# First attention stage of a four-stage decoder kernel: largest scores ahead of P's split, P turned right behind the value products, row tiles turned by VectorE and transfers instead of TensorE

## The reference

```
x = x + tanh(g_xattn[0]) * L0_xattn(layernorm(x), ctx)   # attention, 16 heads in 8 pairs
x = x + tanh(g_ffn[0])   * L0_ffn(layernorm(x))          # feed-forward with 8 low-rank experts, top 2
x = x + tanh(g_xattn[1]) * L1_xattn(layernorm(x), ctx)   # causal attention
x = x + tanh(g_ffn[1])   * L1_ffn(layernorm(x))          # mixture of 8 low-rank maps

# L0_xattn, for a batch b of 128 rows and a head h (Wq, w_kc_q, W_qr folded to one 512x64 matrix A_h):
q_r    = x_b @ A_h                     # 128 x 64
k_r    = rope(ctx_b) @ W_kr[h]         # 128 x 64
P      = softmax(q_r @ k_r.T)          # 128 x 128
out_b += P @ rope(ctx_b) @ G_h         # G_h = w_kc_kv[h].T @ Wo's rows of h: 128 x 512
```

## Time and profile before

| | |
|---|---|
| median of 3 runs | 1375.35 us (1373.85 to 1378.79) |
| the profiled execution | 1376.7 us, of which the span is 1374.9 us |
| granted TensorE clock, mean | 0.997 of full speed |
| busy: PE, DVE, ACT, POOL | 1348.0, 929.3, 518.5, 422.1 us |

### The profile page before, as it was taken

How to read it: one execution, slowest core, us unless ns; L and a number is a source line. 1 busy time by engine, 2 the same in 40 slices (tenths; PEclk the granted TensorE clock), 3 DMA queues, 4 the chain that set the end, 5 groups by cost and what they waited for, 6 DMA issues and landing times.

```text
span 1374.9 us, 20467 instructions
## 1 busy us (share of the span) xinstructions
PE 1348.0 (98%) x7596; PEld 1091.5 (79%) x7596; DVE 929.3 (68%) x1787; ACT 518.5 (38%) x1569; POOL 422.1 (31%) x463
## 2 busy tenths in 40 slices
PE   7899999999999999999999999999999999999999
PEld 6688888888778788878887888788876788887787
DVE  5565675666674877786678667776988777845533
ACT  2544455445464331231113111311127777822220
POOL 3123433233254443101111112113427865630000
PEclk9999999999999999999999999999999999999999
DMA  8633434433454322210121112112334031144431
GB/s 282 222 124 101 148 124 130 131 123 116 135 149 120 92 85 77 88 47 20 43 88 31 51 39 85 43 46 69 106 102 136 28 129 62 47 139 153 139 123 54
DMA packets 108615, 138.35 MB, mean 101 GB/s; under 512 B 12876, under 2 KB 66252, under 8 KB 108516
## 3 DMA queue, kind: packets, MB, share of 16 engines
q1 hardware_dynamic: 108516, 137.05, 31.3%
HBM read 97.15 MB, written 39.85 MB: 100 GB/s over the span
## 4 chain that ended last, share of the span: by engine, by line
PE 81%; DVE 9%; DMA 5%; ACT 2%; issue 1%; SPq 1%; POOL 1%; DVEq 0%; ACTq 0%; POOLq 0%
PE bank L118 78%; PE bank L121 4%; DMA PYZ<-pscr 2%; DMA pscr<-PYZ 2%; SPq L170 1%; DVE PYZ L164 1%; DVE XR L140 1%; DVE AH L130 1%; DVE STG L130 1%; DVE AH L127 1%; DVE st L152 1%; ACT Pb L124 1%; ACT PT L124 1%; DMA XR<-scr 0%; DVE XR L137 0%
## 5 line engine op out<-in xcount | busy, mean ns | idle before, releaser
L118 PE MATMUL bank<-XT,AR 128*128 128x512 f32 x1152 | 280.2, 393 | 0.1
L118 PE MATMUL bank<-AR 128*128 128x512 f32 x1056 | 260.6, 396 | 3.2 <-DVE Msb L127 2.3
L118 PEld LDWEIGHTS bank<-XT,AR 128*128 128x128 f32 x1152 | 213.9, 188 | 48.3 <-issue 1.5
L124 ACT ACTIVATE STG<-bank,b1c 128x512 f32<-128x512 f32 x128 | 88.3, 690 | 387.7 <-PE bank L118 317.7
L118 PEld LDWEIGHTS bank<-AR 128*128 128x128 f32 x1056 | 193.7, 188 | 48.2 <-DVE Msb L127 2.7
L118 PE MATMUL bank<-AR,CT 128*128 128x512 f32 x768 | 192.7, 394 | 0.0
L118 PE MATMUL bank<-AR,AH 128*128 128x512 f32 x768 | 185.9, 390 | 0.0
L127 DVE CAST AH<-STG 128x512 fp32r<-128x512 f32 x192 | 93.8, 488 | 110.5 <-PE bank L118 96.4
L118 PEld LDWEIGHTS bank<-AR,AH 128*128 128x128 f32 x768 | 143.7, 188 | 30.7 <-issue 1.1
L118 PEld LDWEIGHTS bank<-AR,CT 128*128 128x128 f32 x768 | 140.0, 188 | 27.2 <-issue 0.4
L127 POOL CAST BA<-STG 128x256 fp32r<-128x256 f32 x64 | 31.4, 490 | 396.4 <-PE bank L118 242.8
(11 more groups left out here) (139 smaller groups left out, 1839.3 us busy)
## 6 DMA issues: line engine op xcount, KB each, us to landing
XR<-scr SPq DMA_DIRECT2D x64, 256.0 KB, 2.9
pscr<-PYZ SPq DMA_DIRECT2D x30, 512.0 KB, 2.9
PYZ<-pscr SPq DMA_DIRECT2D x120, 128.0 KB, 2.9
XR<-in_x_dram SPq DMA_DIRECT2D x32, 256.0 KB, 3.6
scr<-XR SPq DMA_DIRECT2D x32, 256.0 KB, 2.1
STG<-in_WoT_dram SPq DMA_DIRECT2D x8, 512.0 KB, 3.9
STG<-in_Wq_dram SPq DMA_DIRECT2D x8, 512.0 KB, 4.9
STG<-in_W1L_dram SPq DMA_DIRECT2D x16, 256.0 KB, 2.7
```

Source lines behind the costliest of these rows:

```text
L118: return self.e.matmul(o, w, x, start=start, stop=stop, skip_group_check=True) if self.e else Nothing()
L124: return self.e.activation(o, x, func, **kw) if self.e else Nothing()
```

## The change

Five things change, all in the first stage.

- `by_blocks` also holds for the row tiles of (0, 1), (0, 2), (0, 3) and (1, 0). TensorE's 16 `ln_turn` in the steps (64 transposes) go. VectorE gets `ln_blocks` behind `ln_norm`, SyncE `ln_store`, and one step later `ln_back`; both parts are then made from the SBUF tile `XR` (`ln_split`, p = 4 to 7) and no longer from a PSUM bank. The blocks go through the tile `LNY`, at an address that was a gap.
- VectorE: `scores1` is cut into `largest1` and `inverse1`, and P's low part stands between them. It is that of u-3 at a step's beginning, where it was that of u-2 at a step's end. ScalarE's high part stands first in its step.
- VectorE: `blocks1(u-1)` comes right behind the low parts of `pv1(u-3)`, ahead of the row tile's work and of `final1`.
- VectorE: `ln_norm` moves from a step's beginning to its end, behind `blocks1`.
- SyncE: `p_store` stands ahead of the weights' loads `prep_b(4)` to `prep_b(7)`, and of the stores of finished tiles.

```diff
-            sb("gap", [128, 608], F32, st1)
+            LNY = sb("LNY", [128, 608], F32, st1)
...
         def by_blocks(ph, m):
-            return (ph, m) in ((1, 1), (1, 2), (1, 3), (2, 0))
+            return (ph, m) in ((0, 1), (0, 2), (0, 3), (1, 0), (1, 1), (1, 2), (1, 3), (2, 0))
+
+        def in_stage1(ph, m):
+            return ph == 0 or (ph, m) == (1, 0)
...
         def ly_free(ph, m):
+            if in_stage1(ph, m):
+                if (ph, m) == (0, 1):
+                    return t_ly.sem, 0
+                return t_ly[0, m - 1 if m else 3, 3]
             return xr_free("tail", 1, (m - 1) % 4, 0)
...  (tensor)
-                if u < NU and 3 <= p <= 6:
-                    ln_turn(*after1(m), p - 3, ring4.next())
...  (scalar)
+                if 3 <= u < NU:
+                    split1p(u - 3)
                 if 1 <= u <= NU:
                     scores1(u - 1)
...
-                if u < NU and 3 <= p <= 6:
-                    ln_turn(*after1(m), p - 3)
-                if 2 <= u < NU:
-                    split1p(u - 2)
+                if u < NU and 4 <= p <= 7:
+                    ln_split(*after1(m), p - 4)
                 if u == 31:
+                    split1p(29)
...  (vector)
-                if u < NU and 3 <= p <= 6:
-                    ln_norm(*after1(m), p - 3)
                 if u + 1 < 8:
                     prep_a(u + 1)
                 if 1 <= u <= NU:
-                    scores1(u - 1)
+                    largest1(u - 1)
+                if 3 <= u < NU:
+                    split1p(u - 3)
+                if 1 <= u <= NU:
+                    inverse1(u - 1)
...
                 if 3 <= u < NU:
                     pv1(u - 3, (1,))
+                if 1 <= u < 31:
+                    blocks1(u - 1)
+                if u < NU and 3 <= p <= 6:
+                    ln_norm(*after1(m), p - 3)
+                    ln_blocks(*after1(m), p - 3)
                 if u < NU and p == 7 and m + 1 < NM:
                     kv_turn(m + 1)
-                if u < NU and 3 <= p <= 6:
-                    ln_turn(*after1(m), p - 3)
+                if u < NU and 4 <= p <= 7:
+                    ln_split(*after1(m), p - 4)
...
-                if 2 <= u < NU:
-                    split1p(u - 2)
-                if 1 <= u < 31:
-                    blocks1(u - 1)
...  (sync)
+                if u < NU and 4 <= p <= 7:
+                    ln_back(*after1(m), p - 4)
...
                 if 1 <= u < 31:
                     p_store(u - 1)
+                if u == 1:
+                    prep_b(4)
+                    prep_a(5)
...
+                if u < NU and 3 <= p <= 6:
+                    ln_store(*after1(m), p - 3)
```

More of the change, by code:

```diff
@@ L451, in by_blocks @@
         def by_blocks(ph, m):
-            return (ph, m) in ((1, 1), (1, 2), (1, 3), (2, 0))
+            return (ph, m) in ((0, 1), (0, 2), (0, 3), (1, 0), (1, 1), (1, 2), (1, 3), (2, 0))
+        def in_stage1(ph, m):
+            return ph == 0 or (ph, m) == (1, 0)
         def ly(ph, m):
-            return xr_ap("tail", 1, (m - 1) % 4, 0)
+            return LNY[:, 0:512] if in_stage1(ph, m) else xr_ap("tail", 1, (m - 1) % 4, 0)
         def ly_free(ph, m):
+            if in_stage1(ph, m):
+                if (ph, m) == (0, 1):
+                    return t_ly.sem, 0
+                return t_ly[0, m - 1 if m else 3, 3]
             return xr_free("tail", 1, (m - 1) % 4, 0)
@@ L1558, in prep_b, with largest1 @@
                 lo_of(("A", p), lo, ps.ap(("A", p))[:, :], hi).then_inc(*ps.drain(("A", p), on_dve))
-            def scores1(u):
+            def largest1(u):
                 for j in range(2):
@@ L1569, in scores1, with inverse1 @@
                     e.ts(S[:, 0:4], S[:, 0:4], -1.0, None, ALU.mult, None).then_inc(*nb_ok.mark((u, j)))
+            def inverse1(u):
                 for j in range(2):
@@ L1726, in vector @@
                     ln_pre(*after1(m), p - 2)
-                if 2 <= u < NU:
-                    split1p(u - 2)
-                if 1 <= u < 31:
-                    blocks1(u - 1)
+                if u == 31:
+                    split1p(29)
                 if u in (31, 32):
@@ L2342, in sync @@
             prep_a(4)
-            prep_b(4)
-            prep_a(5)
             for u in range(NU + 3):
                 m, p = divmod(u, 8)
+                if u < NU and 4 <= p <= 7:
+                    ln_back(*after1(m), p - 4)
                 if u < NU and 2 <= p <= 4:
@@ L2351, in sync @@
                     p_load(u - 2)
[L2352 to L2360, removed]
                 if u >= 32:
                     ba_load(u - 32)
-                if u >= 4 and (u - 4) % 8 == 7 and u < NU:
-                    for b in (2, 3):
-                        x_store("fin", 0, (u - 4) // 8, b, ("acc", (u - 4) // 8, b))
                 if u == 8:
@@ L2381, in sync @@
                     p_store(u - 1)
+                if u == 1:
+                    prep_b(4)
+                    prep_a(5)
+                if u == 2:
+                    prep_b(5)
+                    prep_a(6)
+                if u == 3:
+                    prep_b(6)
+                if u == 4:
+                    prep_a(7)
+                if u == 5:
+                    prep_b(7)
+                if u < NU and 3 <= p <= 6:
+                    ln_store(*after1(m), p - 3)
+                if 4 <= u < NU and (u - 4) % 8 == 7:
+                    for b in (2, 3):
+                        x_store("fin", 0, (u - 4) // 8, b, ("acc", (u - 4) // 8, b))
                 if 3 <= u < NU and (u - 3) % 8 == 7:
```

## The result

| kernel | median, us | runs | profiled execution: time / span, us |
|---|---|---|---|
| before | 1376.08 (1373.85 to 1378.79) | 5 | 1376.7 / 1374.9 |
| changed | 1366.89 (1364.96 to 1368.96) | 5 | 1366.0 / 1364.2 |
| changed, again beside another set of runs | 1364.49 (1362.96 to 1366.50) | 6 | 1366.1 / 1364.3 |

The ratio is 0.9932 with an interval of 0.9916 to 0.9949; the second time it is 0.9917 (0.9902 to 0.9932). Both lie inside the forecast. The gain is 9.2 us between the medians and 10.7 us between the two spans. Of the spans' difference, steps 1 to 30 give 11.8 us (380.96 against 369.16, from the first K,Q group of step 1 to that of step 31); 0.7 us are lost ahead of step 1 and 0.4 us behind the start of step 31.

A forecast was written before the change was run, and what follows sets the result against it. TensorE, busy 98% of the span, was taken as the bound; 6.6 + 6.0 + 4.5 = 17.1 us freed, less 0.3 and 5.5, gives 11.3 us. Forecast 1364 us against the median 1375.35, range 1357 to 1370.

The forecast's parts named there:

- transposes out, 16 tiles: First stage, TensorE: turned tiles go at 0.44 us each, 6.6 us for 15, the one in step 3 counted there.
- step 3, beside its tile: Step 3, 20.95 us long: gain of 6.0 us with its turned tile, from shorter TensorE waits; bounds 3 and 7.2.
- late largest scores: Mainly steps 27 to 30: TensorE's waits go as largest scores start earlier, 4.5 us freed.
- new waits: P's low part late at p = 3, 0.3 us; VectorE slowed beside GpSimd in steps 15, 23, 29, 30, 5.5 us.
- step 3 stays: Rival: in step 3 weights and P share the queues, only 3 us of the 6 come; 1367 us, chance 0.12.
- gain 6.0: Step 3: 7.23 us to be had, less 0.7 for P's low part and 0.5 for banks of the second exponentials.
- steps 15 and 23: Sign: TensorE waits there for P's low part or exponentials, with steps 29 and 30 some 5 us; 1.0 us each.
- ScalarE's wait for `PYZ<-pscr`: Sign: ScalarE's wait for P's transfer is gone in the profile after.
- no contention: Rival: no contention with GpSimd worth naming, 17.1 us less; 1358 us, chance 0.17.
- P's load late: Rival: SyncE's order makes `p_load` late at p = 4 to 7, 0.5 us in 16 steps; 1372 us, chance 0.06.
- VectorE the bound: Rival: first `pv1` waits for P's low part in all 16 steps with a row tile; 1383 us, chance 0.05.

The follow-up runs named there:

- x2: The changed kernel with the first stage's row tiles turned by TensorE again, the new order of P's parts and of SyncE's weights kept; 1375.43 us, ratio 1.0008.
- x3: The changed kernel with SyncE's loads of weights ordered as before the change, prep_b(4) and prep_a(5) ahead of the loop, later ones behind p_load; 1365.49 us.
- x4: The changed kernel with prep_b(4) and prep_a(5) moved from step 1 to step 2, behind the first row tile's load and p_load(0); 1363.71 us.
- x7: The changed kernel with GpSimd's low parts of the feed-forward weights in steps 28 to 31 cut to one column of 512, the rest not computed; 1362.24 us.
- x5: The changed kernel with the largest score written negated by the reduction itself, so the first stage's 64 separate negations go; 1365.63 us.
- x8: The changed kernel with VectorE turning the blocks of every first-stage row tile twice, at the end of steps with p = 3 to 6; 1374.05 us.
- x1: The changed kernel with the order of P's parts as before, row tiles still turned by VectorE and transfers; 1413.76 us, ratio 1.0275.
- x9: The changed kernel unaltered, run once more on the same chip as the others; 1364.49 us.
- x6: The changed kernel with weights of pair 4 and the first of pair 5 loaded behind p_load(0), and largest scores negated by the reduction; 1359.84 us, ratio 0.9883.

## Why the prediction was right, term by term

In us of steps 1 to 30, taken from the step lengths:

| term | forecast | measured |
|---|---|---|
| transposes out, 16 tiles | 7.0 | 7.0 |
| step 3, beside its tile | 5.6 | 2.8 |
| late largest scores | 4.5 | 5.6 |
| new waits | -5.8 | -3.8 |
| sum | 11.3 | 11.6 (11.8 by the ends) |

The mechanism held: TensorE's step is what counts, the transposes came off it in full, and what is given back is given back where P's low part is late. But three sizes were off. Late largest scores gave 1.1 us more and the new waits took 2.0 us less than forecast, which cancelled the 2.8 us that step 3 lacked. That the sum is within half a microsecond is luck; the measured 1367 was the forecast's number for the rival *step 3 stays*.

- **Transposes.** Steps of p = 3, 5 and 6 are 11.64 us, but for 29 and 30. x2 gives the other side: with the transposes on TensorE these steps are back at 12.08.
- **Late largest scores.** What was above 12.08 in steps 11, 12, 19, 20 and 27 to 30: 0.30, 0.44, 0.30, 0.46, 1.47, 0.44, 0.79, 1.44, in sum 5.6. I had read steps 27 to 30 well and put what the others lose at 0.4, where it is 1.5. x2 shows that this isn't all the new order's: with the transposes still on TensorE it takes away 2.6 us of the 5.6. The other 3.0 come only when the turned tile goes as well.
- **Step 3, mis-sized: the term "gain 6.0".** 3.2 us came with the tile's 0.44. I took everything above 13.72 us, 7.23 in all, for time in which TensorE stands still. By the table of step 3 it was 3.6 us of waits, 0.4 of the tile, 2.7 of work at the lower clock, and 0.5 because the undisturbed step is 14.2 and not 13.7. I let 1.2 us of it stand; 1.9 us of idle time and 1.6 of lower clock stood. The step that failed is that the clock was put at nothing, and that P was taken to land in time. The term also assumed that P and the tile land no later than before, with 3 us "if the loads of weights, now issued later, are waited for". That is what happened, though the loads were not what was waited for: they stood in front of what was. x3 and x4 gave 2.2 and 3.0 us of it back, 0.7 and 1.4 of this by the wait and the rest by the clock. (The terms of VectorE's work in that passage add up to 5.3 us, so to its 55.1; the 55.8 beside it is no sum of them.)
- **New waits, mis-sized.** At p = 4 it is 0.32 us each and not 0.1; x7 showed that this is the tail's own length. Steps 29 and 30 cost 1.17 each and not 1.4 and 2.1, and x7 and x5 showed that they are GpSimd's. Steps 15 and 23 cost nothing, where I had 1.0 each: behind p = 6 there are no statistics of a next tile, and that room of a microsecond takes the contention, which did occur. Step 7 cost 0.49, which I had called covered; x3 showed that it is the rope of ctx.

The rope of ctx, beside which the forecast saw the tile's low part slow down, and the victims in step 15, from the timeline of the changed kernel:

```profile
209.45 1.30 POOL L130 TENSOR_TENSOR kvr<-MSK,cs 128x512 f32<-128x512 f32 x1 [2.88 <-DMA MSK<-in_ctx_dram]
...
211.70 1.16 DVE L130 TENSOR_TENSOR XT<-XR,XT 128x512 fp32r<-128x512 f32 x1
...
213.49 0.54 DVE L136 TENSOR_SCALAR sm<-sm 128x4 f32<-128x4 f32 x1
```

Of the signs that the forecast named, four came short: no wait came in steps 15 and 23, step 3 was to be about 15 us, steps of p = 4 are 11.96 and not 11.64, and ScalarE's wait for `PYZ<-pscr` was to be gone, where 6.4 us are left. Of the rivals, *no contention* is out (29 and 30, ended by x5 and x7), and *step 3 stays* is half true: its loss of 3 us came, and smaller losses than expected elsewhere made up for it. *P's load late* is out: the waits of ScalarE for it fell from 14.3 to 6.4 us. *VectorE the bound* is out for this kernel, but x8 shows how near it was: 0.73 us more in the tail cost 6.6 us. By the forecast's price (harmless up to 0.5 us, then 16 times the rest) it would have been 3.7, so the room was smaller than I had it. The worst case wasn't on the list: x1, the tiles turned by VectorE without the new order of P, is 2.75% slower, and x2, the new order alone, changes nothing that the medians tell, though its profile has 6 us less in the steps. In the medians the two parts of the change pay only together.

**Settled from the traces.** From the start of step 31 on, profiled spans differ by up to 3.3 us (963.2 to 966.6) between kernels whose code is the same there. The clock has a part in it again. In before, changed, x9, x7 and x8, which took 963.2 to 964.1, it never fell there, but for 0.3 us at the end of before. In x3, x4, x5 and x6, which took 965.6 to 966.6, it stood at 0.50 once, for 3.4 us (an estimate from this: 1.7 us lost); in x3, x4 and x6 this came right behind a wait of 1.9 to 2.3 us for a row tile, which ended at 1283 to 1290 us. x2 (966.0) has 2.3 us more idle time than the changed kernel and only 1.4 us at a lower clock, at its end. So a part of what a change gains can be lost in code that it doesn't touch, and two profiles are compared step by step and not by their spans.

**Left open.** That wait for a row tile was 0.96 us before and 2.08 in the changed kernel, in the same place and with unchanged code; the variants have 1.5 to 2.3 us. I didn't try to find out why, nor why the clock falls behind some of these waits and not behind others.

## What to carry to other kernels

Moving work off the engine that bounds pays by its full time there, but only while what it lengthens elsewhere still has room: walk the engine's tail from its last fixed point to the instruction that is waited for, and count everything that stands in between. A value that goes through store, load, split and back to the next store is a ring: add up all that stands in it on every in-order queue, loads that belong to others included, and compare the sum with the step. Then look for the next ring: here there was one. Read the granted clock of a step before you count its excess as waits: a part of it can be work at the lower level, and it goes or stays with the waits. When a store moves ahead of loads, look at what now stands between it and its own load.

## What the runs showed of the hardware

- A `TENSOR_SCALAR` of 128x4 on SBUF took 0.18 us unhindered and up to 1.27 us beside GpSimd's fp32 `TENSOR_TENSOR`s of 128x512. Reductions from PSUM (0.68) and block transposes in SBUF (0.71) beside them did not change. Writing the negated largest score from the reduction itself took away the victim. A `TENSOR_TENSOR` with both inputs in SBUF is a victim too: 1.18 instead of 0.65 us for 128x512, in step 7.
- Five loads with 1.7 MB, issued between a store and its load, put the landing 4.3 us behind the start of step 3 (54.73 - 50.47); with these loads behind it, it was there at the start (49.30 against 49.27).
- Behind TensorE's waits in step 3 (1.81 us in the changed kernel, 1.11 and 1.42 in x5, 2.33 in x8) the granted clock was 0.50 for a while, from 57.4 to 60.8 us in the changed kernel, and 14.2 us of work took 15.8. It did not fall behind 0.50 us (x4), and not behind every longer wait: in x7 (1.69) and x2 (1.81) it stayed at 1.00.
- VectorE turns 128x512 fp32 in blocks in 0.71 us, and two in a row in 1.46 us; four transposes of such a tile cost TensorE 0.44 us.
